# Identity products in front of four waits of TensorE in the two cross attentions

## What is computed

```python
x = x + _L0_attn_ref(_layernorm(x), ...)                      # "band" stage
x = x + _L0_xattn_ref(_layernorm(x), ctx_1024, mask, mask, ...) # cross0
x = x + _L0_ffn_ref(_layernorm(x), ...)                       # "ffn"
x = x + _L1_attn_ref(_layernorm(x), ...)                      # "self"
x = x + _L1_xattn_ref(_layernorm(x), ctx_1024, ctx_1024, ...) # cross1
x = x + _L1_ffn_ref(_layernorm(x), ...)                       # "moe"
```

## Time and profile before

| | |
|---|---|
| three runs | 2810.91, 2818.48, 2821.30 us (median 2818.48) |
| the profiled execution | 2812.32 us, span of its trace 2810.5 us |
| granted TensorE clock, mean over the span | 0.962 |
| busy: PE, DVE, ACT, POOL | 91%, 69%, 47%, 40% |

### The profile page before, as it was taken

How to read it: one execution, slowest core, us unless ns; L and a number is a source line. 1 busy time by engine, 2 the same in 40 slices (tenths; PEclk the granted TensorE clock), 3 DMA queues, 4 the chain that set the end, 5 groups by cost and what they waited for, 6 DMA issues and landing times. The chain is left out here.

```text
span 2810.5 us, 50716 instructions
## 1 busy us (share of the span) xinstructions
PE 2571.2 (91%) x16973; PEld 1551.5 (55%) x16989; DVE 1928.8 (69%) x3654; ACT 1322.4 (47%) x2007; POOL 1132.5 (40%) x853
## 2 busy tenths in 40 slices
PE   7997899999967899999999999999889999749998
PEld 4775333333335556565656565656444444448997
DVE  5776798998778765657575756566477776665555
ACT  2433477666668643434343434333245554443333
POOL 3323433333047253535453535444454443152333
PEclk9999799999979999999999999999989999859999
DMA  5001322222111000000000000000133332246665
GB/s 171 0 0 40 78 66 62 64 72 59 32 60 46 1 2 2 1 1 1 2 1 1 1 2 1 2 1 1 52 83 86 77 84 71 55 155 229 218 214 194
DMA packets 105254, 160.71 MB, mean 57 GB/s; under 512 B 30877, under 2 KB 65704, under 8 KB 99432
## 3 DMA queue, kind: packets, MB, share of 16 engines
q1 hardware_dynamic: 100056, 148.01, 18.4%
q0 software_dynamic: 3408, 8.46, 0.8%
q10 hardware_dynamic: 1600, 1.61, 0.2%
HBM read 91.66 MB, written 14.96 MB: 38 GB/s over the span
## 5 line engine op out<-in xcount | busy, mean ns | idle before, releaser
L1647 ACT ACTIVATE self_PT<-self_ST 128x1024 f32<-128x1024 f32 x256 | 263.0, 1027 | 483.1 <-PE self_ST L1586 480.5
L1667 DVE TENSOR_REDUCE self_nmax<-self_SM 128x2 fp32r<-128x1024 f32 x256 | 313.1, 1223 | 199.1 <-PE self_SM L1569 198.5
L1735 POOL TENSOR_TENSOR self_U<-self_PT 128x1024 f32<-128x1024 f32 x64 | 153.1, 2392 | 498.5 <-ACT self_PT L1647 498.5
L496 DVE TENSOR_REDUCE cross_nmax<-cross_S 128x2 f32<-128x1024 f32 x256 | 307.5, 1219 | 47.0 <-PE cross_S L350 44.9
L1738 POOL TENSOR_TENSOR self_U<-self_U,self_PT 128x1024 f32<-128x1024 f32 x128 | 303.9, 2374 | 82.2 <-ACT self_PT L1647 80.0
L441 ACT ACTIVATE cross_PT<-cross_S 128x1024 f32<-128x1024 f32 x256 | 259.9, 1025 | 124.4 <-PE cross_S L361 124.0
L1596 PE MATMUL self_W<-self_PT,self_V 128*64 128x512 f32 x1024 | 233.8, 598 | 0.0
L1141 DVE TENSOR_REDUCE cross_nmax<-cross_S 128x4 f32<-128x1024 f32 x128 | 156.5, 1223 | 92.7 <-PE cross_S L968 91.6
L1078 ACT ACTIVATE cross_PT<-cross_S 128x1024 f32<-128x1024 f32 x128 | 131.1, 1024 | 128.0 <-PE cross_S L984 127.7
L1596 PEld LDWEIGHTS self_W<-self_PT,self_V 128*64 128x64 f32 x1024 | 67.8, 136 | 131.8 <-issue 115.6
L1569 PE MATMUL self_SM<-self_k_hi,self_q_hi 64*128 64x512 f32 x512 | 117.7, 456 | 22.9 <-DVE self_nmax L1667 20.1
(11 more groups left out here) (450 smaller groups left out, 6893.6 us busy)
## 6 DMA issues: line engine op xcount, KB each, us to landing
moe_staged<-in_L_ffn_W SPq DMA_DIRECT2D x36, 1024.0 KB
cross_ks<-cross_parts SPq DMA_DIRECT2D x384, 64.0 KB, 2.3
cross_qs<-cross_parts SPq DMA_DIRECT2D x376, 64.0 KB, 2.3
all_x<-in_L_ffn_W SPq DMA_DIRECT2D x14, 1024.0 KB
all_x<-sorted_rows SPq DMA_DIRECT2D x83, 130.0 KB, 2.2
cross_cT<-in_ctx_T SPq DMA_DIRECT2D x16, 512.0 KB, 4.6
sorted_rows<-all_spare_row SPq DMA_DIRECT2D x1, 5460.0 KB, 23.8
all_x<-in_x SPq DMA_DIRECT2D x8, 512.0 KB, 9.2
```

The costliest lines, as they stand in the source:

```text
L496: dve.tensor_reduce(nmax[:, g % 2, 0:R, n % PER_G], S[:, slot[st], :, :], AX.X, ALU.max, negate=True).then_inc(s_maxed, 1)
L1647: act.activation(PT[:, k, :, :], ST[:, :, :], ACT.Exp).then_inc(exped.sem, 1)
L1667: dve.tensor_reduce(nmax[:, i:2 * NT:NT], SM[:, :, :], AX.X, ALU.max, negate=True).then_inc(maxed.sem, 1)
L1735: pool.tensor_tensor(U[:, c % 2, :, :], PT[:, 0, :, :], PT[:, 1, :, :], ALU.add).then_inc(added.sem, 1)
```

## The change

In front of four steps of PE's program, `idle_products` issues matmuls of the identity by itself (128 x 128, fp32) into bank 0 of slot 0 of `S`. Nothing reads the product, nothing is signalled, and PE waits for nothing before them: the wait that the step has stands behind them. There are 16 and 9 in cross0 and 18 and 14 in cross1, 57 in all.

```diff
@@ spread_attention @@
+    IDLE = {('norm', 0, 0): 16, ('qk', 0, 2, 0): 9}
...
+            def idle_products(count):
+                for _ in range(count):
+                    pe.matmul(S[:, 0, 0, 0:P], ident, ident, start=True, stop=True)
+
             for st in pe_steps:
                 kind, b, n = st[:3]
+                if st in IDLE:
+                    idle_products(IDLE[st])
                 if kind == "max":
...
@@ window_attention @@
+    IDLE = {('norm', 0, 0): 18, ('norm', 1, 0): 14}
...
+            def idle_products(count):
+                for _ in range(count):
+                    pe.matmul(S[:, 0, 0, 0:P], ident, ident, start=True, stop=True)
+
             for st in pe_steps:
                 kind, b, n = st[:3]
+                if st in IDLE:
+                    idle_products(IDLE[st])
                 if kind in COVERS:
```

## The result

The changed kernel takes 2831.7 us (median of five runs, 2828.5 to 2835.9), the kernel before 2813.2 (median of five, 2810.9 to 2821.3). The ratio is 1.0054, with a 95% interval from 1.0037 to 1.0072: slower by half a per cent, some 15 us (the medians are 18.5 us apart). The forecast was 2813 us with a range from 2802 to 2821, so it was wrong, and not by a little: between the two profiled executions lie 18.0 us, seven times the 2.5 us of the sum and on the other side.

What follows compares the result with a forecast made beforehand. PE was taken to set the steady pace, with half-clock stretches in the cross attention openings after idles. Gains of 0.5 us in cross0 and about 2.0 in cross1, off a 2815.8 us mean, gave 2813 us, range 2802 to 2821.

Steps and rivals of the forecast that it cites:

- the sum: Whole kernel: likeliest gains of 0.5 us in cross0 and about 2.0 in cross1, together 2.5 us.
- the part on the products' cost: Four PE waits in the cross attention openings: 13.3 us of products fit into them at full clock, so cost nothing.
- Price of a product: PE in the four waits: each product makes two records of 0.117 us at full clock, so 0.23 us.
- the third rival: Products in the four waits dearer, 0.8 us each, overrunning them: slower by 11 us, 2827 us; chance 0.08.
- Idle left: PE behind the products in the four waits: 2.8, 1.4, 2.0 and 2.2 us still idle.
- First wait of cross0: Before cross0's first transposes: a kept clock brings first scores 1.8 us sooner, but 2.8 us idle loses it, 4 in 5.
- Second wait of cross0: Before cross0's projections: clock holds through them, then a 3.5 us idle loses it; 0.5 us won.
- Cross1: Two waits in cross1's opening: kept clocks worth 1.3 and 2.8 us, one of them holds, so about 2.0.
- That a clock held in the opening moves the stage's end by as much: Both cross attentions: PE sets the steady pace (55.26 of 57 us busy in cross0), so opening gains move the stage's end.
- My range: Whole kernel, 2802 to 2821 us: lower end if the clock holds through both openings, upper if no change, slow runs.

Runs made afterwards that it cites:

- loop_longer: Kernel before with 200 already fulfilled waits (100 instructions) at the end of the self attention loop's body, nothing added ahead; 2903.9 us.
- pad_80: Kernel before, no products, with 40 one-column matmuls (80 instructions) at the head of PE's program in cross0; 2822.8 us.
- pad_88: Kernel before, no products, with 44 one-column matmuls (88 instructions) at the head of PE's program in cross0; 2828.7 us.
- only_cross0: Changed kernel with the products of cross1 taken out, those of cross0 (16 and 9) kept; 2832.7 us.
- pad_100: Kernel before, no products, with 50 one-column matmuls (100 instructions) at the head of PE's program in cross0; 2830.0 us.
- pad_356: Kernel before, no products, with 178 one-column matmuls (356 instructions) at the head of PE's program in cross0; 2828.2 us.
- hold_clock: Changed kernel plus 12 products before the eighth maximum of batch 0 in cross0, into a free bank of W; 2809.8 us against 2814.6 of the kernel before, ratio 0.9981.
- only_cross1: Changed kernel with the products of cross0 taken out, those of cross1 (18 and 14) kept; 2814.4 us against 2816.4 of the kernel before, ratio 0.9993.
- all_plus_12: Changed kernel plus 6 one-column matmuls (12 instructions) in front of cross0; 2814.0 us against 2816.4 of the kernel before, ratio 0.9989.
- fuller: hold_clock with more products: 24 and 14 in cross0, 25 and 22 in cross1; 2810.0 us against 2814.4 of the kernel before, ratio 0.9981.

## Why the prediction was wrong

**The step that failed** stands in the part on the products' cost: "At full clock all four fit, so they cost nothing. No engine waits for them, no DMA is issued, no queue is passed". It counts PE's time and the other engines, and leaves out that an instruction also takes a place in PE's program. The 25 products of cross0 are 100 instructions ahead of the loop of the self attention, and they moved its head from 107 instructions ahead of the end of its block to 7. Term of the sum: 0 us; measured: +18.3 us in self, 21.4 in the self attention. "No DMA is issued" was wrong to the letter as well: instructions come by DMA, and q8 moved 7 packets more, 6 of them in the loop.

**The mechanism, as far as it is shown.** The stop comes at an instruction that moves with the padding and returns after 256. The packets of q8 show what happens around it. The 66 taken branches of this loop in before and in all kernels but loop_longer behave alike, with or without a stop: a packet starts 0.9 to 1.6 us into the branch, and the branch ends 1.3 to 1.5 us after that packet has landed; a second packet starts 0.7 to 1.3 us after the branch's end. In the 36 turns that stop (pad_80, pad_88 and the four at distance 7) PE issues again 1.2 to 1.6 us after this second packet has landed, 2.9 to 3.7 us after the branch's end, wherever the instruction stands in the program. Read together: the branch waits for the block of the head, which is hidden by queued matmuls; the next block is asked for only behind the branch; PE works through what lies between in less time than it takes to come, if that is 27 instructions or fewer. The Trainium skill (Runtime: NRT & Kernel Launch, "Instruction fetch mechanics") has the first half of this, that a branch breaks the fetch in sequence; that a second block is late as well, and that a stop depends on where in its block the head lies, is what these runs add. What a packet holds is not in the trace, so that the two are the head's block and the next is inferred from their times and from the place of the stop.

At what distance the stop vanishes is not known: 27 still has it, 107 hasn't, and nothing between was run. An estimate from the table: from distance 7 to 19 to 27 the mean idle goes from 2.40 to 1.57 to 1.16 us, 0.05 to 0.07 us for each instruction, so it would be gone at some 45 to 50.

The packets also say why five kernels have 137 or 138 of them and the others 131 or 132: the six turns behind a taken branch fetch 10 packets each in after, only_cross0, pad_100 and pad_356, 60 in all, and 59 in loop_longer, where the others fetch 9 each, 54 in all. (138 in place of 137, and 132 in place of 131, are the kernels with 228 or more instructions added outside the loop.) A turn has 1,814 records of PE and its sequencer. With the head 7 ahead of a block's end, 7 + 7 x 256 = 1,799, so the turn ends 15 records into a ninth block; loop_longer, 107 ahead and 1,914 long, ends 15 into it as well; pad_80 ends in its eighth. pad_88 should by this count end 3 records into the ninth and still fetches 9, which no run explains. The tenth packet isn't the cost: pad_80 and pad_88 stop without it, and in after the tenth behind the branch of 1108.45 starts at 1241.29, near the end of the turn, where PE doesn't stop.

**Point by point.**

- Price of a product, 0.23 us: measured 3.81 / 16 = 0.238, 2.17 / 9 = 0.241, 4.26 / 18 = 0.237 and 3.29 / 14 = 0.235. Right, and with it the third rival fell: nothing was overrun. It alone had forecast a slower kernel, for a reason that did not come true.
- Idle left: 2.8, 1.4, 2.0 and 2.2 us told; 2.60, 1.53, 1.88 and 2.33 measured.
- First wait of cross0: most likely lost, "4 in 5". It was: the clock fell at 271.51, 0.44 us after work had resumed behind 2.60 us of idle. By the rule of the Trainium skill (TensorE: Matmul & The Clock Gate, "Why this matters for your kernels") that the prediction weighed, no idle of over about 3 us, it would have held; this fall, and the 11 behind the 24 stops of 1.8 to 2.7 us, disagree with that rule again.
- Second wait of cross0: the clock held through the projections, then came the idle that I had derived, "about 3.5 us", measured 3.46, with the clock at 0.50 from 298.81 to 322.71. Gain told 0.5; the first product with v came 1.8 us sooner in after, and 2.7 in hold_clock, which fills that idle.
- Cross1: one of two clocks was to hold, for 1.3 or 2.8 us. In after both held (1.00 through the window above), and the first product with v came 5.4 us sooner than before (4.8 in only_cross1). With the same products it came at 51.4 us in hold_clock and 52.3 in all_plus_12; in these two and in only_cross1 the clock fell once in the opening. So a part of the 5.4 is chance: without products it varies from 50.9 to 54.9.
- That a clock held in the opening moves the stage's end by as much: this step failed too, for cross1. The five kernels with products there take 414.6 to 417.9 us for the stage, the seven without 414.3 to 420.8, and both have the mean 416.8. What the openings win is lost behind them: from 60 us into the stage on the clock is at 0.50 for 6.8 to 13.7 us with products and for 0 to 3.4 without. In cross0 the products of the change leave 514.0 to 514.8 us where the kernels without have 514.7 to 515.2; hold_clock and fuller reach 510.6 and 511.3. One such late fall of cross0 is that at 745.96 (windows above); the 3.40 us ahead of it hold 2.52 us of PE's work.
- The net of all this, without the stop, is all_plus_12: -3 us, or 0.11%, where 2.5 was told. That is agreement within a wide interval (0.6 to 5.9 us), and partly luck: the 2.0 us told for cross1 show in its opening, more than twice over, but not in the length of the stage.

**My range** took its bounds from the waits that the products stand in. Each of them was priced, and no bound was put on what the edit does to code behind it.

## What to carry to other kernels

An edit has two effects: what the instructions do, and where they push the rest of their engine's program. If a later part of that engine's program is a loop of many blocks (this one has about 1,814 instructions a turn), look at the waits of the engine at the head of the loop, before the edit and after: a new row "<- issue" there, equal in each turn, is the second effect. The test is cheap: add a dozen instructions of one column ahead and see whether the time comes back. And compare stages before reading the part that was edited, since here the page and the edited parts showed a success. Of two versions that differ by under 1%, one has to know this alignment before crediting anything else: only with the stop gone could it be seen that the products win 0.1 to 0.2%, and the best two here (hold_clock, fuller) win 0.19%, some 5 us.

## What the hardware showed beyond that

A taken branch of PE doesn't always cost 3.5 us. The two other loops of the kernel, of about 270 and 360 PE instructions a turn (28.9 and 20 us long), have taken branches of 0.21 to 0.24 us in the same trace of before; only the loop of some 1,814 has them of 3.3 to 3.6 us. In the shorter of the two no packet of q8 starts between the first branch and the last, in any trace, and in the other at most one in its twelve turns; the loop of 1,814 has 9 or 10 a turn. So the branch is cheap where nothing is fetched behind it. Between 360 and 1,814 no run shows where that ends.

A stop of 2.2 to 2.6 us costs more than itself: in after four of six were joined by a fall of the clock of 3.4 us, one of them (1114.6) within the stop. Over the four kernels at distance 7 it is 11 of 24.
